# Scores of a cross-attention from four stacks of rounded and remainder rows, three batches ahead, in place of two stacks of plain rows, two batches ahead

## The chip, the core and the metric

The kernel runs on one core of a Trainium2 chip. The metric is the time on the device, in microseconds (us), of one execution. TensorE (PE) multiplies and has a weight load beside it (PEld); VectorE (DVE), ScalarE (ACT) and GpSimd (POOL) do the rest; SyncE (SP) issues most DMAs.

## What is computed

Four layers over `x` (16 batches of 128 rows of 128) with a context of 16 x 120 rows: a cross-attention with 16 heads of 8, a mixture of 16 experts of which each row takes 4, a second cross-attention with one head, and a feed-forward layer whose two square maps are butterflies. All of the change lies in the first:

```python
q = (x @ Wq.T + bq).reshape(B, N, HEADS, HEAD_DIM).transpose(0, 2, 1, 3)
k = (context @ Wk.T + bk).reshape(B, M, HEADS, HEAD_DIM).transpose(0, 2, 1, 3)
v = (context @ Wv.T + bv).reshape(B, M, HEADS, HEAD_DIM).transpose(0, 2, 1, 3)
attn = jax.nn.softmax(jnp.einsum('bhnd,bhmd->bhnm', q, k) * scale, axis=-1)
out = jnp.einsum('bhnm,bhmd->bhnd', attn, v)
return out.transpose(0, 2, 1, 3).reshape(B, N, C) @ Wo.T + bo
```

Here `x` has been normed by row, HEADS is 16, HEAD_DIM 8, N 128, M 120. `x` then gets `tanh(g) * out` added and goes to the mixture.

## The kernel before

Every engine has one program written out by hand, and waits on semaphores. The batches form four groups of four (`G`, `GB`). There are three stages.

The start (0 to about 41 us). For each group PE computes keys (`keys0`), keys and values for the second attention (`keys1`, `both_values`), turns the normed rows (`turn_rows0`) and computes queries (`queries`); ACT takes each from its bank into SBUF. DVE has the row statistics (`row_stats0`, `variances`, `refined`) and norms the rows (`normed_rows`), with a square root on POOL between them (`inverse_root`). At the end of that DVE writes two small sums of the identity (lines 1333 and 1334, semaphore `sums_rdy`); POOL waits for them and makes from them the butterflies' first matrices (lines 356 to 398, semaphore `up_mats`). PE multiplies these (`products(..., UP_L)`, line 1022) between its first score phases.

A score is a product over 8 numbers. Keys and queries of a group leave PE as 128 partitions by columns. `stack_k` and `stack_q` fold them by DMA into `ks` and `qs`: in each of four blocks of 32 partitions 8 rows hold the 8 numbers of a head, a ninth (row `HD`) holds one for the keys and minus the row's maximum for the queries, and the rest is zero. `ks` and `qs` have room for two groups. Groups 0 and 1 are stacked from SP (half of group 0's queries from ACT) at the start. Groups 2 and 3 are stacked from POOL, in its program order: `stack(2)` stands behind the weight splits `split(0)`, `split(1)`, the bias rows `xr` and all of the second butterfly's matrices, `stack(3)` behind `split(2)` and `split(3)`; each also waits until the batches that used its half are done (`st_mm`).

The attention loop (41 to about 135 us, 16 batches). `phase(b, half)` on PE holds 16 matmuls that compute the scores of batch b transposed, for the exponential (line 931), and between them 16 that compute the scores of batch b + 2, for the maxima (line 938); both have 32 rows and 120 or 128 columns, in fp32. DVE takes the maxima (`maxima`, line 1347), PE turns them (`turn_max`, line 946), ACT copies them to `mxr` (line 694), and SP's `stack_max` (line 288) carries them by DMA to the ninth row of `qs`, for which `phase(b, 0)` waits (`mx_ld`). Then come `values` (line 957), `turn_heads` (966), `weighted` on DVE, `turn_attn` (973), `project` (977) and `residual` on DVE (1361). In one iteration PE does: phase(b, 0), turn_max(b + 1), values(b - 1), turn_attn(b - 2), phase(b, 1), project(b - 2), turn_heads(b - 1). `keep_busy` (line 1003) is a matmul of no use, with 256 columns.

POOL, after `stack(3)`, does the rest of the first butterfly (lines 406 to 412), `up_bias_stages`, `values1` four times (line 487), `norm2(0)` (lines 499 to 513) and `norm_rows(0)` (518, 520). The last gives the rows that PE turns in iteration 14 with `turn_normed(0)` (line 983).

The mixture and what follows (135 to 354.5 us) need `up` (lines 1105 to 1107), whose weights are the splits: `w1_hi` (rounded) and `w1_lo` (remainder), for which PE waits with `w1_split`. Each split is a cast and a subtraction of 128 x 1024 on POOL (lines 430, 431), with the fetch of the next but one behind it (line 330).

## Time and profile before

| | us |
|---|---|
| median of 3 runs | 356.65 (356.06 to 357.22) |
| the profiled execution | 356.27 |
| its span, first to last instruction | 354.5 |
| PE busy in the span | 314.1 (89%) |
| DVE, ACT, POOL busy | 240.3, 211.8, 159.5 |

Between the profiled execution and its span lie 1.8 us. The busy shares are means over stages with different limits, so what a change of one stage is worth is read in that stage: in the list of instructions in order of time, in the waits of a stretch, and in the clock granted to PE there.

### The profile page before, as it was taken

The numbers are of one execution on the slowest core, as the hardware profiler recorded it, in microseconds if no ns is written. First come the engines' busy times: TensorE is split into PE (matmuls) and PEld (weight loads), VectorE is DVE, ScalarE is ACT, GpSimd is POOL, SyncE is SP. The second block draws the span as 40 slices with busy tenths as digits, with TensorE's granted clock in tenths as the row PEclk, the third lists the DMA queues.
The fourth block names the chain that finished last, engine by engine and source line by source line (L and its number), as shares of the span: only waits on it lengthen the run. The fifth ranks groups of instructions, "written<-read, shape, count | busy, mean of one in ns | idle before, by whom it ended". The sixth has DMA issues, their size and how long they took to land.

```text
span 354.5 us, 7313 instructions
## 1 busy us (share of the span) xinstructions
PE 314.1 (89%) x2654; PEld 222.9 (63%) x2654; DVE 240.3 (68%) x603; ACT 211.8 (60%) x411; POOL 159.5 (45%) x254
## 2 busy tenths in 40 slices
PE   4768998839798998999999978999889998999986
PEld 2435777637677776666666645765656665646866
DVE  5672556625566464969998978788958888758251
ACT  3545366615456576685658666668676566764733
POOL 3358998991998021317936340046200394312020
PEclk9999999969899999999999999999999999999999
DMA  7958220120430004323322223413223332000100
GB/s 232 201 70 186 74 66 4 32 35 4 66 121 7 6 2 138 134 89 112 131 93 87 91 88 86 124 46 108 90 92 115 92 108 97 5 1 3 59 31 30
DMA packets 15091, 27.93 MB, mean 79 GB/s; under 512 B 2552, under 2 KB 4040, under 8 KB 15048
## 3 DMA queue, kind: packets, MB, share of 16 engines
q1 hardware_dynamic: 12720, 23.00, 22.2%
q0 software_dynamic: 1408, 3.18, 4.1%
q10 hardware_dynamic: 928, 1.29, 1.3%
q8 instruction: 21, 0.34, 0.4%
q14 instruction: 14, 0.11, 0.1%
HBM read 24.05 MB, written 1.18 MB: 71 GB/s over the span
## 4 chain that ended last, share of the span: by engine, by line
PE 51%; POOL 14%; DVE 13%; issue 8%; ACT 8%; DMA 5%; SPq 1%; ACTq 0%; DVEq 0%; POOLq 0%
PE bank L1116 10%; PE bank L1105 5%; PE bank L1107 5%; PE bank L1106 5%; PE bank L1226 4%; PE bank L931 4%; PE bank L957 3%; PE bank L1211 3%; DMA x_sb<-in_x 3%; DVE rings L1533 3%; DVE rings L1536 2%; POOL xr L442 1%; POOL w_lo L431 1%; DMA rings<-mxr 1%; ACT rings L792 1%
## 5 line engine op out<-in xcount | busy, mean ns | idle before, releaser
L1105 PE MATMUL bank<-xhl,w_hi 128*128 128x512 f32 x128 | 74.9, 585 | 0.8 <-ACT rings L792 0.8
L792 ACT ACTIVATE rings<-bank,cols 128x512 f32<-128x512 f32 x64 | 44.1, 689 | 49.2 <-PE bank L1107 48.9
L1347 DVE TENSOR_REDUCE nt<-bank 128x4 f32<-128x480 f32 x64 | 39.9, 650 | 40.0 <-PE bank L938 40.0
L1533 DVE SCALAR_TENSOR_TENSOR rings<-rings,gates 128x512 f32<-128x512 f32 x64 | 47.4, 740 | 16.9 <-ACT rings L792 16.6
L1107 PE MATMUL bank<-xhl,w_hi 128*128 128x512 f32 x128 | 50.5, 394 | 0.0
L1106 PE MATMUL bank<-xhl,w_lo 128*128 128x512 f32 x128 | 50.3, 393 | 0.0
L931 PE MATMUL bank<-rings,ks 32*120 32x128 f32 x512 | 38.4, 289 | 10.5 <-DMA rings<-rings 6.4
L796 ACT ACTIVATE rings<-bank,b1c 128x512 f32<-128x512 f32 x64 | 44.0, 688 | 0.5
L931 PEld LDWEIGHTS bank<-rings,ks 32*120 32x120 f32 x512 | 32.3, 186 | 15.9 <-issue 12.4
L938 PE MATMUL bank<-ks,rings 32*128 32x120 f32 x512 | 38.9, 291 | 1.3 <-DVE nt L1347 0.7
L1105 PEld LDWEIGHTS bank<-xhl,w_hi 128*128 128x128 f32 x128 | 24.1, 188 | 18.1 <-ACT rings L792 7.9
L1106 PEld LDWEIGHTS bank<-xhl,w_lo 128*128 128x128 f32 x128 | 24.2, 189 | 17.1 <-issue 14.4
L938 PEld LDWEIGHTS bank<-ks,rings 32*128 32x128 f32 x512 | 32.8, 194 | 2.2 <-DVE nt L1347 1.3
L1116 PE MATMUL bank<-rings,x_sb 128*128 128x512 f32 x64 | 33.1, 598 | 0.0
L1536 DVE TENSOR_SCALAR rings<-rings 128x512 f32<-128x512 f32 x64 | 33.0, 515 | 0.1
L1116 PE MATMUL bank<-wide,x_sb 128*128 128x512 f32 x64 | 32.7, 592 | 0.0
L1107 PEld LDWEIGHTS bank<-xhl,w_hi 128*128 128x128 f32 x128 | 24.0, 187 | 5.7
L533 POOL TENSOR_TENSOR xhl<-xnt,xhl 128x512 fp32r<-128x512 f32 x4 | 5.7, 1422 | 48.3 <-ACT xhl L709 27.1
L1541 DVE TENSOR_TENSOR rings<-rings 128x512 f32<-128x512 f32 x32 | 24.2, 757 | 4.2
L1541 DVE TENSOR_TENSOR wide<-rings 128x512 f32<-128x512 f32 x32 | 22.8, 713 | 4.6 <-DVE rings L1536 0.5
L339 POOL TENSOR_TENSOR cs<-cs,minus_half 128x4 f32<-128x4 f32 (+1 forms) x5 | 7.2, 1437 | 34.9 <-DVE cs L1292 34.9
L685 ACT ACTIVATE wide<-bank 120x512 f32<-120x512 f32 x32 | 17.1, 584 | 6.0 <-PE bank L931 6.0
(247 smaller groups left out, 625.9 us busy)
## 6 DMA issues: line engine op xcount, KB each, us to landing
gates<-gate_rows SPq DMA_DIRECT2D x64, 256.0 KB, 3.1
bw<-in_L_ffn_w POOLq DMA_DIRECT2D x4, 512.0 KB, 5.3
x_sb<-in_x SPq DMA_DIRECT2D x4, 256.0 KB, 7.7
x_sb<-in_L_ffn_w SPq DMA_DIRECT2D x2, 512.0 KB, 4.3
wide<-in_ctx ACTq DMA_DIRECT2D x4, 240.0 KB, 6.8
out<-xr SPq DMA_DIRECT2D x3, 256.0 KB, 2.1
gates<-in_flies SPq DMA_DIRECT2D x1, 704.0 KB, 7.0
rings<-rings POOLq DMA_DIRECT2D x8, 64.0 KB, 4.5
```

The source lines that it names most:

```text
L792: act.activation(esg[:, e % 2, :], SB[1 + e % 2][:, :], ACT.Gelu_apprx_sigmoid, bias=b1_in[:, 0, e:e + 1]).then_inc(s["m_sg"], 1)
L796: act.activation(eb[:, e % 2, :], (SB[3], PK)[e % 2][:, :], ACT.Identity, bias=b1c[:, e:e + 1]).then_inc(s["m_eb"], 1)
L931: mm = pe.matmul(turned_bank(b, gg)[0:M, r * P:(r + 1) * P], ks[32 * gg:32 * gg + 32, i, r, mc], qs[32 * gg:32 * gg + 32, i, r, tc], start ...
L938: mm = pe.matmul(score_bank(ahead, n)[:, r * M:(r + 1) * M], qs[rows32, ia, r, ta], ks[rows32, ia, r, ma], start=True, stop=True)
L1105: pe.matmul(bk[:, :], w1_hi[:, e, branch, :], low(g), start=True, stop=False)
L1106: pe.matmul(bk[:, :], w1_lo[:, e, branch, :], high(g), start=False, stop=False)
L1107: pe.matmul(bk[:, :], w1_hi[:, e, branch, :], high(g), start=False, stop=True).then_inc(s[done], 1)
L1116: pe.matmul(Y[:, :], w2_sb[:, e, :], es[e % len(es)], start=False, stop=(e == E - 1), skip_group_check=True).then_inc(s["m_y"], 1)
L1347: dve.tensor_reduce(nt[:, b % 2, OF[n], :], score_bank(b, n)[:, 0:HR * M].rearrange("p (r m) -> p r m", r=HR), AX.X, ALU.max, negate=True) ...
L1533: dve.scalar_tensor_tensor(eq[:, j, :], esg[:, j, :], GELU_LIMIT, gates[:, (n - 1) % NG, :], ALU.min, ALU.mult).then_inc(s["m_eq"], 1)
L1536: dve.tensor_scalar(ec[:, j, :], eb[:, j, :], LIMIT + 1.0, 1.0 - LIMIT, ALU.min, ALU.max).then_inc(s["m_ec"], 1)
L1541: dve.tensor_tensor(es[e % len(es)], eq[:, j, :], ec[:, j, :], ALU.mult).then_inc(s["m_s"], 1)
```

## The change

Each group gets stacks of its own. Keys of groups 0 and 1 lie in `w1_lo`, queries of groups 0 and 1 in `w1_hi`, keys of groups 2 and 3 in `ks`, queries of group 2 in `xhl`, of group 3 in a new `qs`. Every number now has four rows: rounded keys, rounded keys, the keys' remainder and (in the last number's place, `MAX_ROW`) the row of the maximum, against rounded queries, the queries' remainder, rounded queries. So 24 rows and one more of each 32 are used. The matmuls stay in fp32 with 32 rows. DVE computes the remainders (`low_keys`, `low_queries`, eight instructions). A stack is filled by six DMAs of 240 or 256 KB, each to every fourth partition, all from SP; groups 2 and 3 are stacked in the first batches of the loop, after POOL has filled and zeroed their slots. Since the slots lie in the weights' tiles, POOL splits all four quarters of the weights only once batch 7 is through (`halves`). Scores are computed three batches ahead of their use instead of two. Six `keep_busy` are added in the last batches. The probabilities of the second attention and two hidden tiles of the last layer move to other tiles (`p1`, `p1t`, `hid`; not shown).

```diff
 
 
+    MAX_ROW = 3
+    AHEAD = 3
...
-        ks = sb("ks", [P, 2, HR, GB * M])
+        ks = sb("ks", [P, 2, HR * GB * M], F32R)
...
+        qs = sb("qs", [P, HR * GT], F32R)
...
-        kt_row = sb("kt_row", [P, G, GB * M])
...
+        KSLOT, QSLOT = HR * GB * M, HR * GT
+        k_rows = (w1_lo_row[:, 0:KSLOT], w1_lo_row[:, KSLOT:2 * KSLOT], ks[:, 0, :], ks[:, 1, :])
+        q_flat = (w1_hi_row[:, 0:QSLOT], w1_hi_row[:, QSLOT:2 * QSLOT],
+                  xhl[:, :, :].rearrange("p s c -> p (s c)"), qs[:, :])
+        k_slot = [v.rearrange("p (r u m) -> p r u m", r=HR, u=GB) for v in k_rows]
+        q_slot = [v.rearrange("p (r u t) -> p r u t", r=HR, u=GB) for v in q_flat]
+        q_lo = ring_row[:, 0:2 * GT].rearrange("p (i t) -> p i t", i=2)
+        k_lo = ring_row[:, 2 * GT:2 * GT + 2 * GB * M].rearrange("p (i t) -> p i t", i=2)
+        kt_row = ring_row[:, 4 * GT:4 * GT + G * GB * M].rearrange("p (g t) -> p g t", g=G)
...
+        def stacked(eng, slot, row, src, landed):
+            eng.dma_start(slot[row:P:4].bitcast(F32), src).then_inc(s[landed], 16)
...
-            sp.wait_ge(s["ks_fill"], 1)
-            sp.wait_ge(s["kt_rdy"], 1)
-            stack_k(sp, 0, range(HG))
+            def stack_k(g):
+                if g < 2:
+                    sp.wait_ge(s["ks_fill"], g + 1)
+                else:
+                    sp.wait_ge(s["kb_fill"], g - 1)
+                sp.wait_ge(s["kt_rdy"], g + 1)
+                stacked(sp, k_slot[g], 0, kt_row[:, g, :], f"ks_ld{g}")
+                stacked(sp, k_slot[g], 1, kt_row[:, g, :], f"ks_ld{g}")
+                sp.wait_ge(s["kl_rdy"], g + 1)
+                stacked(sp, k_slot[g], 2, k_lo[:, g % 2, :], f"ks_ld{g}")
+
+            def stack_q(g):
+                sp.wait_ge(s["qs_zero"], g + 1)
+                sp.wait_ge(s["qt_rdy"], g + 1)
+                stacked(sp, q_slot[g], 0, q_rows[g], f"qs_ld{g}")
+                stacked(sp, q_slot[g], 2, q_rows[g], f"qs_ld{g}")
+                sp.wait_ge(s["ql_rdy"], g + 1)
+                stacked(sp, q_slot[g], 1, q_lo[:, g % 2, :], f"qs_ld{g}")
...
+            stack_k(0)
             sp.dma_start(flies, a["flies"]).then_inc(s["ld_fly"], 16)
-            sp.wait_ge(s["qs_zero"], 1)
-            sp.wait_ge(s["qt_rdy"], 1)
...
-            stack_k(sp, 1, range(HG))
+            stack_q(0)
+            stack_k(1)
             sp.dma_start(mats[:, W_T, :].rearrange("p (c d) -> p c d", c=HC), a["L1_ffn_W_exp"]).then_inc(s["ld_exp"], 16)
...
-            stack_q(sp, 1, range(HG))
+            stack_q(1)
...
             def stack_max(b):
                 sp.wait_ge(s["mxr_rdy"], b + 1)
-                sp.dma_start(qs[HD:P:32, (b // GB) % 2, :, b % GB * P:(b % GB + 1) * P], mxr[:, b % 2, :]
+                sp.dma_start(q_slot[b // GB][MAX_ROW:P:32, :, b % GB, :].bitcast(F32), mxr[:, b % 2, :]
                              ).then_inc(s[f"mx_ld{b % 2}"], 16)
 
             for b in range(NB):
                 stack_max(b)
+                if b in (0, 2):
+                    stack_k(2 + b // 2)
+                if b in (1, 3):
+                    stack_q(2 + b // 2)
...
-            pool.memset(qs[:, 0, :, :], 0.0).then_inc(s["qs_zero"], 1)
+            pool.memset(q_flat[0].bitcast(F32), 0.0).then_inc(s["qs_zero"], 1)
...
-            pool.memset(qs[:, 1, :, :], 0.0).then_inc(s["qs_zero"], 1)
+            pool.memset(q_flat[1].bitcast(F32), 0.0).then_inc(s["qs_zero"], 1)
...
+            for g in range(2, G):
+                pool.tensor_copy(k_rows[g], which[:, MAX_ROW:MAX_ROW + 1].to_broadcast([P, KSLOT])).then_inc(s["kb_fill"], 1)
+                pool.memset(q_flat[g].bitcast(F32), 0.0).then_inc(s["qs_zero"], 1)
...
-            split(0)
-            split(1)
...
-            def stack(g):
-                pool.wait_ge(s["ks_fill"], 2)
-                pool.wait_ge(s["kt_rdy"], g + 1)
-                pool.wait_ge(s["qt_rdy"], g + 1)
...
-            stack(2)
-            split(2)
-            split(3)
-            stack(3)
...
+
+            def halves():
+                pool.wait_ge(s["st_mm"], 2 * GB * HG)
+                for q in range(NQ):
+                    split(q)
...
             up_bias_stages()
+            halves()
             for i in range(G):
...
-                act.activation(kt_row[:, g, :], bank[4][:, 0:GB * M], ACT.Identity,
+                act.activation(kt_row[:, g, :].bitcast(F32R), bank[4][:, 0:GB * M], ACT.Identity,
...
             keys0(2)
             queries(0)
-            act.wait_ge(s["qs_zero"], 1)
-            act.wait_ge(s["qt_rdy"], 1)
-            stack_q(act, 0, range(HG // 2, HG))
...
@@ -728,13 +734,14 @@
             act.wait_ge(s["consts"], 1)
             turned_max(0)
             taken("up_mm1", mats[:, HALFWAY, :], PO[:, :], "up_ev1")
+            turned_max(1)
...
                     taken("ub_mm2", ubx[:, 0, :], PO[:, 0:HC], "ub_rdy")
-                if b + 1 < NB:
-                    turned_max(b + 1)
+                if b + 2 < NB:
+                    turned_max(b + 2)
...
-                    pe.wait_ge(s["kt_rdy"], g)
+                    pe.wait_ge(s["kl_rdy"], g)
...
                 if g >= 1:
-                    pe.wait_ge(s["qt_rdy"], g)
...
-                ahead = b + 2
+                ahead = b + AHEAD
...
-                    i, mc, tc = rows_of(b)
+                    k_, q_, u = k_slot[b // GB], q_slot[b // GB], b % GB
...
                     if ahead % GB == 0 and half == 0:
-                        pe.wait_ge(s[f"ks_ld{ahead // GB}"], 16 * HG)
-                        pe.wait_ge(s[f"qs_ld{ahead // GB}"], 16 * (HG + ahead // (2 * GB)))
+                        pe.wait_ge(s[f"ks_ld{ahead // GB}"], 16 * 3)
+                        pe.wait_ge(s[f"qs_ld{ahead // GB}"], 16 * 3)
                     need(pe, "nt_rdy", ahead * HG + 2 * half - 1)
...
-                            mm = pe.matmul(turned_bank(b, gg)[0:M, r * P:(r + 1) * P], ks[32 * gg:32 * gg + 32, i, r, mc],
-                                           qs[32 * gg:32 * gg + 32, i, r, tc], start=True, stop=True)
+                            mm = pe.matmul(turned_bank(b, gg)[0:M, r * P:(r + 1) * P], k_[32 * gg:32 * gg + 32, r, u, :].bitcast(F32),
+                                           q_[32 * gg:32 * gg + 32, r, u, :].bitcast(F32), start=True, stop=True)
...
-                            mm = pe.matmul(score_bank(ahead, n)[:, r * M:(r + 1) * M], qs[rows32, ia, r, ta],
-                                           ks[rows32, ia, r, ma], start=True, stop=True)
+                            mm = pe.matmul(score_bank(ahead, n)[:, r * M:(r + 1) * M], qa[rows32, r, ua, :].bitcast(F32),
+                                           ka[rows32, r, ua, :].bitcast(F32), start=True, stop=True)
...
             def turn_max(b):
                 pe.wait_ge(s["nt_rdy"], (b + 1) * HG)
-                need(pe, "x1_rdy", b - 3)
+                need(pe, "mxr_rdy", b)
+                need(pe, "x1_rdy", b - 4)
...
             def values(b):
 
                 pe.wait_ge(s["exp_rdy"], (b + 1) * HG)
                 pe.wait_ge(s["v_st"], b + 1)
                 need(pe, "on_rdy", b)
+                if b >= NB - AHEAD:
+                    keep_busy(PO, 1)
...
             def turn_attn(b):
                 pe.wait_ge(s["on_rdy"], b + 1)
-                pe.wait_ge(s["mxr_rdy"], min(b + 4, NB))
+                pe.wait_ge(s["mxr_rdy"], min(b + 5, NB))
                 need(pe, "x1_rdy", b)
+                if b >= NB - AHEAD:
+                    keep_busy(TP, 1)
                 pe.transpose(TP[:, 0:P], on[:, :, :].rearrange("p h d -> p (h d)"), ident[:, :]).then_inc(s["on_turned"], 1)
...
-            phase(-2, 0)
+            phase(-3, 0)
...
+            pe.wait_ge(s["ql_rdy"], G)
+            phase(-3, 1)
+            phase(-2, 0)
             pe.wait_ge(s["v_rdy"], 2 * G)
             turn_max(0)
...
             products(PO, UP_L, lambda c: chunk(W_T, c), "up_mm1")
             keep_busy(bank[3], 1)
+            phase(-2, 1)
+            phase(-1, 0)
+            turn_max(1)
             phase(-1, 1)
-            pe.wait_ge(s["kt_rdy"], G)
+            pe.wait_ge(s["kl_rdy"], G)
             pe.wait_ge(s["bo_rdy"], 1)
...
                 phase(b, 0)
-                if b + 1 < NB:
-                    turn_max(b + 1)
+                if b + 2 < NB:
+                    turn_max(b + 2)
...
+            dve.tensor_copy(k_rows[0], keys_of).then_inc(s["ks_fill"], 1)
+
+            def low_keys(g):
+                dve.wait_ge(s["kt_rdy"], g + 1)
+                if g >= 2:
+                    dve.wait_ge(s[f"ks_ld{g - 2}"], 16 * 3)
+                dve.scalar_tensor_tensor(k_lo[:, g % 2, :].bitcast(F32R), bank[4][:, 0:GB * M], bcol[:, CK0:CK0 + 1],
+                                         kt_row[:, g, :], ALU.add, ALU.subtract).then_inc(s["kl_rdy"], 1)
+
+            def low_queries(g):
+                dve.wait_ge(s["qt_rdy"], g + 1)
+                if g >= 2:
+                    dve.wait_ge(s[f"qs_ld{g - 2}"], 16 * 3)
+                dve.scalar_tensor_tensor(q_lo[:, g % 2, :].bitcast(F32R), bank[2][:, :], bcol[:, CQ0:CQ0 + 1],
+                                         q_rows[g], ALU.add, ALU.subtract).then_inc(s["ql_rdy"], 1)
...
             row_stats0(0)
             own.wait()
             variances(GB, stats[:, 0:GB, :], mean[:, 0:GB])
-            dve.tensor_copy(ks[:, 1, :, :], keys_of).then_inc(s["ks_fill"], 1)
+            dve.wait_ge(s["ld_kb"], 16)
+            low_keys(0)
+            dve.tensor_copy(k_rows[1], keys_of).then_inc(s["ks_fill"], 1)
             for g in range(1, G):
                 row_stats0(g)
             refined(1, GB, rr[:, 0:1, 0:GB])
             normed_rows(0)
             own.wait()
             variances(NB - GB, stats[:, GB:NB, :], mean[:, GB:NB])
+            low_keys(1)
             refined(2, NB - GB, rr[:, 0:1, GB:NB])
-            for g in range(1, G):
-                normed_rows(g)
+            normed_rows(1)
+            low_queries(0)
+            low_keys(2)
+            normed_rows(2)
+            normed_rows(3)
+            low_queries(1)
+            low_keys(3)
             own.mark(dve.tensor_reduce(in_block, ident[:, :].rearrange("p (b j) -> p j b", b=NBLK), AX.X, ALU.add))
             dve.tensor_reduce(of_block, ident[:, :].rearrange("p (b j) -> p b j", b=NBLK), AX.X, ALU.add).then_inc(s["sums_rdy"], 1)
...
             maxima(0, 0)
             maxima(0, 1)
+            low_queries(2)
+            low_queries(3)
             row_bias()
             maxima(0, 2)
             maxima(0, 3)
+            for n in range(HG):
+                maxima(1, n)
             for n in range(HG - 1):
-                maxima(1, n)
+                maxima(2, n)
             for b in range(NB + 2):
-                if b + 1 < NB:
-                    maxima(b + 1, HG - 1)
+                if b + 2 < NB:
+                    maxima(b + 2, HG - 1)
                 if b >= 2:
                     weighted(b - 2)
-                if b + 2 < NB:
+                if b + AHEAD < NB:
                     for n in range(HG - 1):
-                        maxima(b + 2, n)
+                        maxima(b + AHEAD, n)
```

## Rows read from the trace of the kernel before

**Rows 1.** The page, first line: the span.
```profile
span 354.5 us, 7313 instructions
```
**Rows 2.** Waits between 66 and 80 us: who waited for whom, us, times, longest.
```profile
PE bank L931 <- DMA rings<-rings: 6.4, 1, 6.4
```
**Rows 3.** Chain that ended last, 60 to 135 us: start, us, what.
```profile
89.33 4.58 DMA rings<-mxr
```
**Rows 4.** DVE in order of time: `residual` of one batch; start, us, instruction.
```profile
69.93 0.34 DVE L1361 SCALAR_TENSOR_TENSOR xr<-bank,tg,xr 128x128 f32<-128x128 f32 x1
...
82.48 0.34 DVE L1361 SCALAR_TENSOR_TENSOR xr<-bank,tg,xr 128x128 f32<-128x128 f32 x1
...
92.31 0.34 DVE L1361 SCALAR_TENSOR_TENSOR xr<-bank,tg,xr 128x128 f32<-128x128 f32 x1
...
99.84 0.34 DVE L1361 SCALAR_TENSOR_TENSOR xr<-bank,tg,xr 128x128 f32<-128x128 f32 x1
...
119.50 0.34 DVE L1361 SCALAR_TENSOR_TENSOR xr<-bank,tg,xr 128x128 f32<-128x128 f32 x1
```
**Rows 5.** Stretches: window, length, busy us by engine, PE's granted clock, DMA share, GB/s.
```profile
76.00:79.00 3.00, 2.67 (x41) 2.25 (x45) 0.57 (x1) 0.25 (x2) 2.86 (x3) 0.50 0.00 0
...
94.00:96.00 2.00, 2.00 (x33) 1.79 (x33) 0.03 (x1) 0.00 (x0) 1.84 (x3) 0.50 0.12 12
```
**Rows 6.** DVE in order of time, 18 to 40 us.
```profile
21.59 3.17 DVE L1311 TENSOR_SCALAR rings<-x_sb,mean,rr 128x128 f32<-128x128 f32 x12
...
24.95 0.28 DVE L1334 TENSOR_REDUCE sums<-ident 128x8 f32<-128x128 f32 x1
```
**Rows 7.** POOL in order of time, 24 to 37 us.
```profile
25.29 0.24 POOL L415 COPY ones_low<-sums 128x64 f32<-128x64 f32 x1 [3.23 <-DVE sums L1334]
...
35.44 1.05 POOL L398 TENSOR_TENSOR mats<-blocks,sums 128x512 f32<-128x512 f32 x1
```
**Rows 8.** SP's queue in order of time: four DMAs of one stack.
```profile
20.37 2.81 SPq L239 DMA_DIRECT2D ks<-kt_row  x4
```
**Rows 9.** The page, DMA issues: KB of each, us from issue to landing.
```profile
bw<-in_L_ffn_w POOLq DMA_DIRECT2D x4, 512.0 KB, 5.3
...
out<-xr SPq DMA_DIRECT2D x3, 256.0 KB, 2.1
```
**Rows 10.** A stretch in which the old stack of group 1 is carried.
```profile
22.00:24.00 2.00, 0.66 (x4) 0.42 (x4) 2.00 (x9) 1.34 (x3) 0.06 (x1) 1.00 0.56 62
```
**Rows 11.** PE in order of time, 33 to 42 us.
```profile
36.12 1.15 PE L938 MATMUL bank<-ks,rings 32*128 32x120 f32 x16 [0.74 <-DVE nt L1347]
...
37.32 1.06 PE L1022 MATMUL bank<-mats 128*128 128x128 f32 x8
38.21 0.60 PE L1003 MATMUL bank<-wt,ident 128*128 128x256 f32 x2
...
41.35 0.36 PE L931 MATMUL bank<-rings,ks 32*120 32x128 f32 x1
```
**Rows 12.** DVE's groups by line and shape: busy us, mean ns.
```profile
L1524 DVE SCALAR_TENSOR_TENSOR xr<-bank,tg,xr 128x512 f32<-128x512 f32 x3 | 2.3, 751 | 1.3 <-PE bank L1226 1.1
```
**Rows 13.** POOL in order of time: two splits, then 60 to 165 us.
```profile
36.56 1.04 POOL L430 CAST w_hi<-bw 128x1024 fp32r<-128x1024 f32 x1
...
40.93 1.05 POOL L430 CAST w_hi<-bw 128x1024 fp32r<-128x1024 f32 x1
...
100.98 4.96 POOL L487 TENSOR_TENSOR v_all<-v_all,rows 120x512 f32<-120x512 f32 x4
...
113.54 1.04 POOL L520 TENSOR_TENSOR xn<-xn,rr 128x512 f32<-128x512 f32 x1
```
**Rows 14.** PE in order of time, 119 to 141 us.
```profile
120.90 0.60 PE L983 MATMUL bank<-ident,xn 128*128 128x128 f32 x4
...
132.78 1.08 PE L957 MATMUL bank<-wide,vst 120*32 120x128 f32 x32 [0.56 <-DVE on L1355]
...
134.53 0.49 PE L977 MATMUL bank<-wt,ont 128*128 128x128 f32 x2 [0.40 <-ACT ont L698]
```

55 lines of the change are left out of this document (15 added, 40 removed).

## The prediction

> **What bounds the kernel now.** I read the page first: PE is busy for 89% of a span of 354.5 us [rows 1], and the change touches only the first 135 us, so the mixture behind them is taken as it is. Then I looked for the places where the attention loop is late. `residual` runs once in a batch, so its starts are the loop's beat [rows 4]: from 99.84 to 119.50 lie four batches, 4.92 us each, and from 82.48 to 92.31 two, again 4.92. But 69.93 to 82.48 is one batch (12.55, too long by 7.6), and so is 92.31 to 99.84 (7.53, too long by 2.6). The waits name the first: PE stood 6.4 us for the DMAs of group 2's stack [rows 2], which POOL issued late. The chain names the second: one DMA of a row of maxima that took 4.58 us [rows 3] while group 3's stack was carried. After each stall PE's clock was at half (0.50, the 1.2 GHz level) [rows 5]; that loss is inside the two excesses. Together the loop loses 10.2 us. That is all that the change can win here: its matmuls keep type, rows and columns.
>
> Then the start. The first loop phase begins at 41.35 [rows 11]. POOL's matrices need 25.29 to 36.49, 11.2 us [rows 7], and POOL begins when DVE has made the two sums, at 25.23 [rows 6]. PE is there at about the same time as the matrices (37.32) [rows 11], so POOL's chain can't slip without being seen.
>
> **The loop, minus 10.2.** All four stacks have slots of their own and SP issues the last two around batches 0 to 3; `phase(5, 0)`, the first to read group 2, comes 25 us after the loop's start (five beats). Both stalls go: the first because nobody waits for POOL, the second because a row of maxima is now turned a whole batch earlier, so its DMA has 4.9 us more. The beat stays 4.92: phase, turn, values and the DVE steps keep their order and only the batch number of the scores ahead changes. In batch 13 the scores ahead fall away; DVE has four maxima less in a batch that it helps to pace. I take 0.5 off (between 0 and 1.0, an estimate), since the 16 matmuls that are left run almost as long.
>
> **The start, plus 8.9.** This is the term that I am least sure of. `low_keys(3)` stands ahead of the two sums on DVE and waits until all three key DMAs of group 1 have landed. Queued behind it on DVE are the sums, and on them wait POOL's matrices, and on these PE. Step by step:
> - `low_queries(0)` comes after `normed_rows(1)`, a third of 3.17 us after 21.59, so at 22.65 [rows 6]. A remainder over 512 columns with one operand in PSUM costs 0.75 by the nearest row [rows 12]; done at 23.4. Eight of these add 6 us to DVE, nearly all in idle time of the start; what they cost is where they wait.
> - SP then issues the last query DMA of group 0 and the three key DMAs of group 1 in its order. An old one takes 0.70 us of SP [rows 8]; the last starts at 25.5.
> - Landing: the near bound is 2.1 us for 256 KB from an idle queue [rows 9], so 27.6. The far bound is volume: these four carry 976 KB, and the old stack ran at 62 GB/s with the engines at 0.56 [rows 10], 111 GB/s if full, thus 8.8 us from 24.5, 33.3. I take 28.6, near the first, because the old DMAs each wrote to 8 neighbouring partitions and the new ones write to 32 spread over all 128.
> - Remainder 0.75 and sums 0.6: POOL starts at 30.0 instead of 25.3, its matrices are ready at 41.2. PE by then has done everything up to `turn_max(0)` by about 38.4 (the remainders of group 3's queries hold its second phase until 35) and idles for some 3 us.
> - From the matrices on, before, it was 4.03 us to the first loop phase (37.32 to 41.35) [rows 11]. Now two more phases stand there, each 1.15 plus 0.74 of waiting for a maximum, 1.89 [rows 11]: 7.8 us, so 49.0. Stalls of this kind cost the clock in two places above; I add 1.2 for it. The loop starts at 50.2, 8.9 late. Bounds: 4.9 late if the matrices come by 38.4 and the clock holds; 14 late at the far bound.
>
> Here the Trainium skill is to be weighed ("SBUF — State Buffer", section on the DMA port swizzle). Its rule is that a DMA's rate grows with how many of 16 ports its partitions reach, and that 8 neighbouring ones reach two, while every fourth of 128 reaches all. With its fit of 2 us plus bytes at 436 GB/s the key DMAs would land at about 27.8 and the start would slip by 0.8 less, for a time of 356.3, called an estimate. The row with 62 GB/s for the old form agrees with the rule's direction; no row shows the new form.
>
> **The end of the loop, plus 2.2.** A `keep_busy` costs 0.60 us of PE [rows 11], and PE does them after its wait, so they lengthen the path. Six make 3.6. PE idles 0.56 and 0.40 there [rows 14], and DVE paces part of it, which may swallow some. I take 2.2, between 0 and 3.6.
>
> **POOL's splits, plus 0.4.** They start after phase(7, 1). What POOL must do until PE can turn the first normed rows in batch 14: two splits with the issue of a fetch behind them at 4.37 (40.93 minus 36.56), two without at 3.5, and 1.2 us of waiting for the two fetches, which take 5.3 each [rows 9, 13]; then values, norms and rows, 100.98 to 114.58, 13.6 [rows 13]. That is 8.7 + 7.0 + 1.2 + 13.6 = 30.5 us. PE needs seven beats less the 2.9 us between a turn and the end of its second phase, less the 0.5 above: 31.1. Before, the rows were ready 6.3 us early (114.58 against 120.90) [rows 13, 14]; now half a microsecond is left. That cover is thin, so 0.4 (0 to 2). The fills and zeroing for groups 2 and 3 and all that POOL moves ahead of the splits end near 80, before batch 7 does (88), and cost nothing.
>
> SP: the key stacks of groups 2 and 3 stand ahead of rows of maxima and wait for POOL's fills (43 to 47). The row of batch 1 is then issued near 47 and needed at 55; nothing.
>
> **Sum.** 356.27 (profiled execution, 1.8 over its span [rows 1]) - 10.2 - 0.5 + 8.9 + 2.2 + 0.4 = 357.1. The profiled execution lies 0.4 under the median 356.65, so this is 0.1% above the median: no change that could be measured. A measurement of this kernel can tell about 0.3% (1.1 us) from none.
>
> **Rivals.**
> - *The matrices hardly slip.* If the key DMAs land by 27.6, something holds DVE less, and the clock holds, the start is 4.9 late and the `keep_busy` are partly swallowed (1.5): 352.0, up to 354.5 between. For it: nothing but small steps has to go right. Against: the sum above has the matrices at 41.2, and this needs 38.4. I give it 0.22, at 352.5.
> - *The key DMAs land late* (slower). Place: DVE's wait in `low_keys(3)`. Each microsecond beyond 28.6 moves the loop by one. At 33 the start is some 13 late: 361.2. It decides from about 30 on. For it: three times the old volume, 1920 byte pieces. Chance 0.13.
> - *The splits are late.* Place: `turn_normed(0)` waiting for POOL in batch 14. Each microsecond beyond 31.1 is paid; with 3 late, 360. It decides if a split takes over 4.5 us or a fetch over 6. Chance 0.12.
> - *The change doesn't do what it says:* a stack or a row of maxima still comes late in batches 1 to 5, since 3 MB pass SP's queue there. With half of the stalls back, 362. Chance 0.05.
> - The forecast, 357.1, own range 355 to 359.5, keeps 0.48: of that 0.10 is faster by over 0.3% (under 355.6), 0.20 within, 0.18 slower.
>
> Faster: 0.22 + 0.10 = 0.32. Same: 0.20. Slower: 0.18 + 0.13 + 0.12 + 0.05 = 0.48. The range goes from 352.3, which cuts off the better half of the first rival, to 361.5, which cuts off half of the second and the fourth.
>
> **What would show it.** In the changed profile: `residual` at a beat of 4.92 from batch 2 to 13 with no gap over 6; the line of the two sums at 29 to 30 instead of 24.7; the last matrix at 41; the first transposed scores at 50, with a clock of 0.50 between; the four splits from about 88; the turning of normed rows with a short wait for POOL. Wrong it would be if the sums come at once (the start then is only bound by PE), if the beat itself changes with the new rows, or if the mixture's 219 us move.

## The result and the profile after

| | before | after |
|---|---|---|
| median of 18 runs each, us | 356.36 | 360.55 (358.20 to 367.17) |
| the profiled execution, us | 356.27 | 359.00 |
| its span, us | 354.5 | 357.2 |
| mean granted clock of it | 0.986 | 0.975 |

The changed kernel is slower: 1.0096 times the kernel before, 95% interval 1.0066 to 1.0126, some 3.4 us. Medians are of all executions; a ratio leaves out slow ones, more than 1.5% above the fastest of their kernel. 357.1 was forecast, in a range of 352.3 to 361.5. The range held, and the forecast lies 3.5 us under the median. The profiled execution of after is one of its better ones, 1.6 us under that median, so the ledger below explains 2.7 us of span and not all of the 4.2 us between the medians.

The page of after, its first line, PE's line and the clock by fortieths of the span (8.9 us each):
```profile
span 357.2 us, 7348 instructions
...
PE 323.5 (91%) x2666; PEld 230.2 (64%) x2666; DVE 246.0 (69%) x611; ACT 212.3 (59%) x411; POOL 154.8 (43%) x240
...
PEclk9999669999999999999999998999999999999999
```
PE is busy for 9.4 us more than before, and the two sixes, from 36 to 54 us, are where much of that comes from: the same matmuls at half the clock.

`residual` on DVE (start, us), to be laid beside [rows 4]: batches 0, 10 and 15 of the kernel before, then batches 0, 10, 11 and 15 of after, where its line is 1395:
```profile
55.17 0.34 DVE L1361 SCALAR_TENSOR_TENSOR xr<-bank,tg,xr 128x128 f32<-128x128 f32 x1
...
114.59 0.34 DVE L1361 SCALAR_TENSOR_TENSOR xr<-bank,tg,xr 128x128 f32<-128x128 f32 x1
...
138.40 0.35 DVE L1361 SCALAR_TENSOR_TENSOR xr<-bank,tg,xr 128x128 f32<-128x128 f32 x1 [2.19 <-PE bank L977]
```
```profile
65.73 0.34 DVE L1395 SCALAR_TENSOR_TENSOR xr<-bank,tg,xr 128x128 f32<-128x128 f32 x1
...
114.90 0.34 DVE L1395 SCALAR_TENSOR_TENSOR xr<-bank,tg,xr 128x128 f32<-128x128 f32 x1
119.62 0.35 DVE L1395 SCALAR_TENSOR_TENSOR xr<-bank,tg,xr 128x128 f32<-128x128 f32 x1 [3.01 <-PE bank L992]
...
140.61 0.35 DVE L1395 SCALAR_TENSOR_TENSOR xr<-bank,tg,xr 128x128 f32<-128x128 f32 x1 [2.62 <-PE bank L992]
```
From batch 0 to batch 10 these are 49.17 us, ten beats of 4.92 with no gap. Before it was 55.17 to 114.59, 59.42: the stalls of 10.25 us are gone, as forecast (10.2). But batch 0 comes 10.56 us later than before. At batch 10 the two kernels are level (+0.31). The end of the loop, with the six fillers (the `keep_busy` matmuls of the last batches), adds 1.90 (batch 15: 138.40 before, 140.61 now, +2.21), and 0.5 comes behind the loop, which makes the 2.7 us of span.

The start, on DVE and POOL, beside [rows 6] and [rows 7]:
```profile
26.89 0.72 DVE L1297 SCALAR_TENSOR_TENSOR rings<-bank,cols,rings 128x480 fp32r<-128x480 f32 x1 [1.03 <-DMA w_lo<-rings]
27.53 0.36 DVE L1367 TENSOR_REDUCE sums<-ident 128x16 f32<-128x128 f32 x1
...
28.14 0.24 POOL L432 COPY ones_low<-sums 128x64 f32<-128x64 f32 x1 [6.96 <-DVE sums L1368]
...
38.25 1.05 POOL L415 TENSOR_TENSOR mats<-blocks,sums 128x512 f32<-128x512 f32 x1
```
`low_keys(3)` waited 1.03 us for the key DMAs, which landed at about 26.9. The matrices are ready at 39.30, 2.81 us later than before, where 4.7 was forecast.

The same on PE, beside [rows 11]:
```profile
36.02 2.07 PE L942 MATMUL bank<-w_lo,w_hi 32*128 32x120 f32 x16 [0.74 <-DVE nt L1381]
39.36 2.08 PE L1031 MATMUL bank<-mats 128*128 128x128 f32 x8 [0.96 <-POOL mats L415]
...
46.20 2.06 PE L942 MATMUL bank<-w_lo,w_hi 32*128 32x120 f32 x16 [0.54 <-DVE nt L1381]
48.19 2.08 PE L1031 MATMUL bank<-mats 128*128 128x128 f32 x8
...
51.05 0.56 PE L935 MATMUL bank<-w_hi,w_lo 32*120 32x128 f32 x1
```
A score phase of 16 matmuls took 1.15 us before and 2.07 here, eight products 1.06 to 1.16 before and 2.08 here. The stretch from 30 to 36, first of the kernel before, then of after (length, busy us by engine, clock, DMA share, GB/s):
```profile
30.00:36.00 6.00, 4.08 (x30) 2.79 (x28) 0.94 (x3) 2.52 (x5) 5.14 (x16) 1.00 0.80 186
```
```profile
30.00:36.00 6.00, 3.20 (x26) 2.04 (x24) 2.03 (x6) 1.80 (x4) 5.28 (x16) 0.98 0.67 205
```
More stretches of after:
```profile
36.00:38.00 2.00, 1.98 (x16) 1.78 (x16) 0.54 (x1) 0.00 (x0) 1.61 (x8) 0.50 0.06 25
...
40.00:42.00 2.00, 2.00 (x9) 1.57 (x8) 0.00 (x0) 0.53 (x1) 2.00 (x2) 0.50 0.02 8
...
44.00:46.00 2.00, 1.36 (x17) 1.06 (x17) 1.32 (x3) 0.30 (x2) 2.00 (x2) 1.00 0.23 84
46.00:48.00 2.00, 1.80 (x16) 1.78 (x16) 0.71 (x2) 0.26 (x2) 2.00 (x3) 0.51 0.08 27
48.00:50.00 2.00, 2.00 (x12) 1.81 (x9) 1.22 (x2) 0.00 (x0) 2.00 (x3) 0.50 1.00 371
```
Twice the clock is at 0.50 (the 1.2 GHz level): from 36 to 42, after 30 to 36 in which PE was busy for 3.20 of 6 us, and from 46 to 52, after 44 to 46 with 1.36 of 2. In the profiled execution of before it was 1.00 from 30 to 52, with PE busy for 4.08 us from 30 to 36.

The splits on POOL, beside [rows 13], and the turn that waits for them, beside [rows 14]:
```profile
89.81 1.04 POOL L451 CAST w_hi<-bw 128x1024 fp32r<-128x1024 f32 x1 [12.68 <-PE bank L935]
...
119.36 1.04 POOL L529 TENSOR_TENSOR xn<-xn,rr 128x512 f32<-128x512 f32 x1
```
That is 30.6 us from the first split to the normed rows (30.5 forecast). PE turned them at 121.01, 0.6 us after they were ready, with no wait.

### The profile page after: what moved, and what is told of

It is laid out like the page before. It is cut to its first block, busy times and chain, and to the rows that moved or that the text cites. A ratio compares the mean times of both kernels' runs of the same rounds, so it can differ in the third digit from the quotient of the medians.

```text
span 357.2 us, 7348 instructions
## 1 busy us (share of the span) xinstructions
PE 323.5 (91%) x2666; PEld 230.2 (64%) x2666; DVE 246.0 (69%) x611; ACT 212.3 (59%) x411; POOL 154.8 (43%) x240
## 3 DMA queue, kind: packets, MB, share of 16 engines
q10 hardware_dynamic: 848, 1.15, 1.0%
## 4 chain that ended last, share of the span: by engine, by line
PE 62%; DVE 15%; issue 9%; ACT 7%; POOL 4%; DMA 2%; SPq 0%; DVEq 0%; ACTq 0%; POOLq 0%
PE bank L1128 11%; PE bank L935 6%; PE bank L1117 6%; PE bank L1118 5%; PE bank L1119 5%; PE bank L970 5%; PE bank L1238 4%; PE bank L1223 3%; DVE rings L1571 3%; DVE nt L1381 2%; DMA x_sb<-in_x 2%; PE bank L942 2%; PE bank L956 2%; PE bank L1031 2%; DVE rings L1574 2%
## 5 line engine op out<-in xcount | busy, mean ns | idle before, releaser
L1128 PE MATMUL bank<-rings,x_sb 128*128 128x512 f32 x64 | 34.0, 613 | 0.0
L942 PE MATMUL bank<-w_lo,w_hi 32*128 32x120 f32 x256 | 21.4, 312 | 3.4 <-DVE nt L1381 2.0
L942 PEld LDWEIGHTS bank<-w_lo,w_hi 32*128 32x128 f32 x256 | 18.2, 214 | 4.9 <-DVE nt L1381 2.6
L691 ACT ACTIVATE rings<-bank 120x512 f32<-120x512 f32 x32 | 17.1, 584 | 6.2 <-PE bank L935 6.2
L935 PE MATMUL bank<-w_hi,w_lo 32*120 32x128 f32 x256 | 19.1, 288 | 1.5 <-DVE nt L1381 1.5
```

Source lines behind the costliest of these rows:

```text
L935: mm = pe.matmul(turned_bank(b, gg)[0:M, r * P:(r + 1) * P], k_[32 * gg:32 * gg + 32, r, u, :].bitcast(F32), q_[32 * gg:32 * gg + 32, r, u ...
L942: mm = pe.matmul(score_bank(ahead, n)[:, r * M:(r + 1) * M], qa[rows32, r, ua, :].bitcast(F32), ka[rows32, r, ua, :].bitcast(F32), start=T ...
L1128: pe.matmul(Y[:, :], w2_sb[:, e, :], es[e % len(es)], start=False, stop=(e == E - 1), skip_group_check=True).then_inc(s["m_y"], 1)
```

## The experiments

Each was timed in five rounds. Four series were run, each with the kernel before beside it (its medians: 356.5 for e1 to e4, 356.6 for e5 to e8, 357.5 for e9 to e11, 356.3 for e12). "Ratio" is that of the times to the kernel before, with its 95% interval. "Clock" is the mean granted clock of the profiled execution, and "batch 0" is where `residual` starts for batch 0 in it. A difference between two medians of different series can be off by about 1 us: the median of the kernel before moved by that much.

| run | median, us | ratio | clock | batch 0 |
|---|---|---|---|---|
| changed kernel | 360.55 | 1.0096 [1.0066, 1.0126] | 0.975 | 65.73 |
| e1 sums first | 360.52 | 1.0117 [1.0076, 1.0159] | 0.975 | 65.80 |
| e2 gaps filled | 354.89 | 0.9967 [0.9938, 0.9996] | 0.995 | 60.96 |
| e3 no fillers at the end | 357.93 | 1.0051 [1.0024, 1.0077] | 0.976 | 65.42 |
| e5 e2 and e3 | 352.39 | 0.9901 [0.9862, 0.9939] | 0.999 | 60.67 |
| e8 e5, values later | 351.76 | 0.9881 [0.9847, 0.9916] | 0.994 | 60.94 |
| e6 two ahead | 353.47 | 0.9913 [0.9879, 0.9946] | 0.984 | 58.67 |
| e9 e6, gaps filled | 350.58 | 0.9841 [0.9798, 0.9883] | 0.995 | 57.16 |
| e10 e9, no fillers at the end | 348.44 | 0.9771 [0.9731, 0.9810] | 0.990 | 57.38 |
| e7 rounded products | 371.90 | 1.0403 [1.0349, 1.0457] | 0.866 | 63.57 |
| e4 before, stack early | 350.02 | 0.9811 [0.9756, 0.9865] | 0.979 | 62.59 |
| e11 the same again | 352.44 | 0.9841 [0.9781, 0.9901] | 0.980 | 62.56 |
| e12 before, gaps filled | 355.90 | 0.9988 [0.9957, 1.0019] | 0.986 | 58.52 |

**e1: is it the slip of the matrices?** The two sums go ahead of the remainders that wait.

```diff
+            own.mark(dve.tensor_reduce(in_block, ...))
+            dve.tensor_reduce(of_block, ...).then_inc(s["sums_rdy"], 1)
             low_queries(1)
             low_keys(3)
-            own.mark(dve.tensor_reduce(in_block, ...))
-            dve.tensor_reduce(of_block, ...).then_inc(s["sums_rdy"], 1)
```

> The changed kernel, with DVE's two sums ahead of the last two remainders instead of behind them. The theory (the late start is the clock's doing, the matrices' slip costs only the 1 us that PE waits for them): POOL begins at about 25 instead of 28.1, the matrices are ready by 36.5, PE waits for them no more, and the first loop phase comes 1 to 1.5 us earlier than at 51.05 with the clock still at its 1.2 GHz level in two stretches; time 359 against 360. The rival (the matrices' chain paces the whole start, as forecast): the first loop phase comes some 2.8 us earlier, near 48; time 357. A third possibility: with the 1 us wait gone the clock doesn't fall the first time, and the gain is 3 or more; then the clock row between 36 and 42 us tells it.

The sums came at 24.48, as early as before, and nothing was gained: 360.52. PE in order of time in this kernel:
```profile
35.28 1.63 PE L942 MATMUL bank<-w_lo,w_hi 32*128 32x120 f32 x16 [3.08 <-DVE rings L1304]
37.64 2.06 PE L942 MATMUL bank<-w_lo,w_hi 32*128 32x120 f32 x16 [0.74 <-DVE nt L1381]
```
The wait for the matrices is replaced by one for the remainders of the queries, now longer (3.08 where it was 1.34), and the clock was at half in the same two places. The edit moved more than the sums. POOL's two weight fetches of 512 KB stand behind them, and were issued at 25.80 instead of 28.84; the last query DMA of group 1, issued at 26.38, then took 8.0 us to landing (3.7 in after), and the remainder of group 3's queries waited for it until 34.47 (33.32 in after). So e1 shows a second chain that is as late as the matrices. It doesn't show that the matrices' slip costs nothing, and e2 and e9 below show that it does cost.

**e2: is it the clock?** Seven fillers go into the gaps.

```diff
+            keep_busy(bank[3], 2)
             pe.wait_ge(s["ql_rdy"], G)
             phase(-3, 1)
+            keep_busy(bank[3], 1)
             phase(-2, 0)
+            keep_busy(bank[3], 1)
             pe.wait_ge(s["v_rdy"], 2 * G)
             turn_max(0)
+            keep_busy(bank[3], 1)
...
             phase(-2, 1)
+            keep_busy(bank[3], 1)
             phase(-1, 0)
+            keep_busy(bank[3], 1)
             turn_max(1)
             phase(-1, 1)
```

> The changed kernel, with seven useless matmuls of 256 columns put into the places between 32 and 47 us where PE waits for maxima, remainders or matrices. The theory (PE's clock falls to its 1.2 GHz level because these early phases are paced by DVE and leave PE idle, and half speed makes the start long): granted clock 1.00 from 34 to 54 us, first loop phase at about 47 instead of 51.05, time 355.5 to 356. The rival (the start is long because two phases, their maxima and the late matrices stand in it, the clock matters little): each filler costs its 0.5 us where it isn't hidden, first loop phase at 51 to 53, time 360 to 362.

Seven matmuls of no use made the kernel 5.6 us faster by the medians (4.6 by the ratios). Stretches of this kernel:
```profile
34.00:40.00 6.00, 4.86 (x46) 3.68 (x47) 2.89 (x6) 0.27 (x1) 5.31 (x13) 1.00 0.07 28
40.00:46.00 6.00, 5.88 (x62) 4.39 (x61) 2.74 (x5) 1.16 (x4) 6.00 (x4) 1.00 0.35 124
46.00:52.00 6.00, 6.00 (x93) 5.06 (x92) 3.18 (x6) 2.95 (x8) 5.89 (x7) 1.00 0.59 218
```
The clock is 1.00 throughout, a phase takes 1.15 us again, and batch 0 comes 4.77 earlier. This shows the cause of the late start beyond the work itself. PE in order of time around the matrices and the three phases behind them:
```profile
39.20 1.16 PE L1035 MATMUL bank<-mats 128*128 128x128 f32 x8 [1.03 <-POOL mats L415]
...
40.73 1.15 PE L942 MATMUL bank<-w_lo,w_hi 32*128 32x120 f32 x16
...
42.62 1.15 PE L942 MATMUL bank<-w_lo,w_hi 32*128 32x120 f32 x16
...
44.52 1.15 PE L942 MATMUL bank<-w_lo,w_hi 32*128 32x120 f32 x16
```
Two things can be read here. With the clock held PE still waits 1.03 us for the matrices, and starts their products 1.88 later than before (39.20 against 37.32 [rows 11]). And the phases are 1.89 and 1.90 us apart with a filler between them, as far apart as the forecast had them without one, so those fillers lie wholly in the gaps.

A small part of the gain is lost again later. PE in order of time in batch 14 of this kernel:
```profile
117.03 0.65 PE L998 MATMUL bank<-ident,xn 128*128 128x128 f32 x4 [0.73 <-POOL xn L529]
```
PE waits for the normed rows behind POOL's splits. POOL's chain took 31.9 us here, since two fetches were waited for (0.92 and 1.61 us; 0.77 and 0.47 in after).

**e3: the six fillers at the end.** The four lines of `keep_busy` in `values` and `turn_attn` are left out.

> The changed kernel without the six useless matmuls in the last three batches. Theory of the forecast (they lie on the path and cost 2.2 us): the first matmul of the mixture comes about 1.8 us earlier after residual(10), the third pair about 2.2, and the time falls to 358. The rival (they hold the clock up): without them the granted clock falls below 1.00 between 118 and 142 us and the time stays at 360 or rises.

357.93, so 2.6 us less. A stretch of this kernel:
```profile
118.00:142.00 24.00, 21.24 (x257) 17.44 (x256) 10.78 (x47) 15.46 (x35) 6.49 (x10) 1.00 0.15 49
```
The clock is 1.00 without them, so in this kernel they kept nothing up. In the profile the stretch from batch 11 to 15 is 1.07 shorter (119.33 to 139.25, against 119.62 to 140.61), with a late chain on POOL once more (32.1 us, and PE waited 0.91 us for it). Between the later pair e9 and e10, where POOL is not late, the same edit gives 2.04 (111.24 to 132.19, against 111.46 to 130.37).

**e5 and e8: both together, and POOL's chain without `values1`.** e5 has the edits of e2 and e3. e8 also has POOL compute `values1` behind `norm_rows(0)`.

> The changed kernel with the early gaps filled and without the six useless matmuls of the last batches: two edits together that gave 5.6 and some 2 us alone. If they add up, 353. The theory of POOL's splits says that they don't quite: with the loop at its full beat the normed rows of batch 14 come late, PE waits 0.7 to 1.3 us for them before it turns them (it was 0.73 with the gaps filled), and the time is 353 to 354.

> The same as e5_gaps_no_tail, with one step moved: POOL adds the bias to the second attention's values (4 x 1.24 us) after the normed rows of group 0 instead of before them. If POOL's chain of splits is what PE waits for in batch 14, the wait goes, residual(11) to residual(12) falls by 1 us or more, and the time is 1 us under e5_gaps_no_tail, 352 to 352.5. The rival (that wait is covered by other work of the last batches, which PE does in its place): both times equal.

352.39: the two gains add up. With `values1` out of the way, the normed rows are ready 4.8 us earlier (111.05 against 115.81), and from batch 11 to 12 it takes 6.62 us where e5 took 6.61. So in e5's profile POOL wasn't on the path (31.1 us from the first split, no wait on PE), and the times of e5 and e8 lie within each other's intervals. This says nothing of executions with later fetches.

**e6: was the third batch ahead needed?**

```diff
-    AHEAD = 3
+    AHEAD = 2
...
-            phase(-3, 0)
+            phase(-2, 0)
...
-            phase(-3, 1)
-            phase(-2, 0)
+            phase(-2, 1)
+            phase(-1, 0)
...
-            phase(-2, 1)
-            phase(-1, 0)
-            turn_max(1)
             phase(-1, 1)
...
-                if b + 2 < NB:
-                    turn_max(b + 2)
+                if b + 1 < NB:
+                    turn_max(b + 1)
```
(`maxima`, `turned_max` and the bounds of the waits go with it; the fillers of the last three batches stay.)

> The changed kernel with scores two batches ahead again instead of three; stacks, rows and useless matmuls of the end as in the change. Theory of the forecast: the third batch costs the start two phases of 1.89 us, and buys only cover for the rows of maxima. So the loop starts at about 46 to 47 instead of 51.05, and PE waits for rows of maxima in batches 1 to 4, while SP's queue carries the stacks of groups 2 and 3; if these waits stay under 4 us in all, the time is 356 to 358. The rival (the cover is needed): waits for rows of maxima of 6 us and more, clock down again in the loop, time 361 or above.

7.1 us less, where no more than 4.5 was expected. The beat is 4.92 from batch 0 to batch 11, and no wait for a row of maxima is among PE's waits: the waits expected in batches 1 to 4 didn't come. SP issues each late stack right behind a row of maxima (the row at 46.55, three query DMAs from 47.23, the next row at 51.69), and no row came late by it. So with these stacks the order didn't have to change. Stretch of this kernel where the clock still falls:
```profile
38.00:42.00 4.00, 3.04 (x13) 2.29 (x11) 1.22 (x2) 0.82 (x3) 3.85 (x4) 0.50 0.01 4
```

**e9 and e10: two ahead with the gaps filled, then without the fillers at the end.** Five fillers: two before the wait for `ql_rdy`, one behind each of the two phases that follow, one behind `turn_max(0)`.

> The changed kernel with two batches ahead instead of three, and five fillers of 128 x 256 in the gaps of its start (in the three-ahead kernel seven such fillers gave 5.6 us). Theory (of the 7 us that two ahead gave, a part was the second fall of the clock and the rest the two phases): one stretch at 0.50 is left in the two-ahead kernel, and in it a phase takes 2.07 instead of 1.15, the products 2.08 instead of 1.16 and the filler 1.06 instead of 0.6. With the gaps filled the clock stays at 1.00 and the first residual row comes at about 56.5 instead of 58.67; the time is about 351.5 us. Rival (the two-ahead kernel waits in its start for POOL's products of matrices and for the remainders of the keys, whatever the clock): the first residual row stays at 58.5 or later and the time at 353.5.

> As the two-ahead kernel with its gaps filled, and without the six fillers of the last three batches. Theory (each of these fillers lies on the path, some 0.3 us each, as it did with three ahead, where leaving them out gave 2.5 us beside the filled gaps): about 2 us less than the same kernel with them, 349.5 us, so 0.98 of the kernel before. Rival (with the score phases of batch 14 and 15 thinner, PE gaps let the clock fall in the last batches): the clock shows 0.5 to 0.8 in the stretch from batch 13 to the first matmul of the mixture, and the time is no less than with the fillers.

350.58 and 348.44: e10 beats both kernels, 0.977 of the kernel before. PE in order of time in e9, the products of the matrices and the first loop phase:
```profile
39.20 1.16 PE L1034 MATMUL bank<-mats 128*128 128x128 f32 x8 [1.03 <-POOL mats L415]
...
43.33 0.36 PE L934 MATMUL bank<-w_hi,w_lo 32*120 32x128 f32 x1
```
With the clock at 1.00 in both, e9 and e2 differ by the third batch ahead and two fillers: 60.96 less 57.16 is 3.80, the very figure forecast for the two phases (e2 shows the two fillers in gaps). In time it is 4.3 us. Batch 0 of e9 is 2.0 behind that of the kernel before. Of that 1.88 is there when PE starts the products of the matrices: with the clock held, the late matrices are all but all that the new stacks cost the start. e9's batch 0 was expected at 56.5 and came at 57.16. Of the fall of the clock that e10's rival expected at the end there was a little (0.93 on the mean of 120 to 140, where e9 has 1.00), and e10 was still 2.1 us faster than e9.

**e7: rounded operands.** In the four operands of the score matmuls `.bitcast(F32)` is left out, so they are read as the rounded type in which they are stored.

> The changed kernel with the score matmuls reading the stacks as the rounded type in which they are stored, instead of as fp32: same rows, same columns, nothing left out. One view (PE's fp32 work is the beat of the loop): the 32 matmuls of a phase, 1.1 us in fp32, take a half or less, and the beat falls from 4.92 to some 4; time 345 or below. The other view (the beat is the ring of DVE's maxima, ACT's exponentials and PE together): the beat falls by less than 0.3, PE has more idle time, the clock falls more often, and the time stays within 2 us of 360.

371.90, so 11.4 us slower than the changed kernel, and outside of both views. A stretch of its loop, then one of PE's groups in 60 to 120 us (busy us, mean ns), and in the third fence the same group of after in 66 to 116:
```profile
60.00:70.00 10.00, 9.87 (x123) 7.33 (x115) 4.91 (x12) 5.84 (x17) 9.53 (x10) 0.50 0.01 3
```
```profile
L970 PE MATMUL bank<-wide,vst 120*32 120x128 f32 x164 | 10.1, 420 | 0.7
```
```profile
L970 PE MATMUL bank<-wide,vst 120*32 120x128 f32 x160 | 5.4, 275 | 1.0 <-DVE on L1389 1.0
```
The beat is 6.02 instead of 4.92 and the clock 0.50 from 60 to 130, nearly to the end of the loop, although PE's row shows it busy for 9.87 of 10 us; `values`, which e7 doesn't touch, has its mean at 420 ns instead of 275. Once down, the loop came back up only behind 130. Why a loop so busy by the profile stays down I can't say: no run tells it apart from other differences of the type, and so the run doesn't show what the rounded type would give with the clock up.

**e4 and e11: the kernel before with one thing moved.**

```diff
+            stack(2)
             own.then_wait(across(wdn_flat, dw2[:, 0, :, :], 2))
             across(wdn_flat, dw2[:, 1, :, :], 1).then_inc(s["dn_crossed"], 1)
             pool.wait_ge(s["dn_crossed"], 1)
...
-            stack(2)
             split(2)
```

> The kernel before, with one edit: on POOL the stack of group 2 stands ahead of the last two steps on the second butterfly's matrices instead of behind them. It isolates the first stall. Theory (the stall of 6.4 us is POOL's program order alone, with the clock behind it): POOL issues the stack at about 61 as soon as batch 3 is through, PE doesn't wait in iteration 6, residual(3) to residual(4) takes 4.9 to 6 us instead of 12.55, and the time falls by some 7 us, to 349.5. The rival (the stack's DMAs, beside the rows of maxima, move the stall to another batch): a wait for a row of maxima of 2 to 4 us appears between 62 and 70, and the gain is 3 to 5 us.

> The kernel before, with nothing of the change but that POOL stacks its last group ahead of the two crossings of the down matrix. Its time is known (350.0 us); wanted is an undisturbed trace of it. Theory (the stalls of the kernel before were POOL's order, not its one stack): from the row of batch 8 to that of batch 9 about 6 us instead of 12.55, of which about 1.6 is a wait for the row of maxima, the first residual row at 55.2 as in the kernel before, and the six stalls of 10.2 us shrunk to some 3.5. Rival (the gain came from elsewhere, the start or the tail): the distances between the rows of batches 0 and 10 are as in the kernel before, and a stretch outside them is shorter.

350.0 and 352.4: two plain stacks with POOL's order mended are 8 to 10.5 us better than the changed kernel, and 0.981 and 0.984 of the kernel before. `residual` in e11, PE's waits in 60 to 110 us, and the issue of group 2's stack by POOL:
```profile
72.39 0.34 DVE L1361 SCALAR_TENSOR_TENSOR xr<-bank,tg,xr 128x128 f32<-128x128 f32 x1
78.38 0.34 DVE L1361 SCALAR_TENSOR_TENSOR xr<-bank,tg,xr 128x128 f32<-128x128 f32 x1
83.30 0.34 DVE L1361 SCALAR_TENSOR_TENSOR xr<-bank,tg,xr 128x128 f32<-128x128 f32 x1
```
```profile
PE bank L931 <- DMA rings<-mxr: 3.2, 2, 1.6
```
```profile
67.64 2.29 POOL L239 DMA_DIRECT2D ks<-kt_row  x4 [6.13 <-PE bank L931]
```
These rows are of batches 2, 3 and 4. From batch 3 to 4, where the kernel before lost 12.55 [rows 4], it is 4.92 here; a gap of 5.99 stands one batch earlier and one of 6.01 from batch 6 to 7, each a wait of 1.6 for a row of maxima. But both profiles caught an execution whose clock had fallen in the start (in e11 0.65 in 26 to 30, 0.63 in 38 to 42, 0.50 in 42 to 46), with batch 0 at 62.6. There POOL, though it waited 6.13 us for batch 3, issued the stack no earlier than in the kernel before (67.84), and PE was late enough not to need it sooner. So the traces don't show the edit at work; its worth is shown by the times. The five executions with a clock of 0.989 or more took 347.5 to 350.9, those near 0.980 took 351.6 to 355.7. And the start of the kernel before can lose its clock too.

**e12: fillers for the kernel before.** The same five as in e9.

> The kernel before with the same five fillers of 128 x 256 in the gaps of its start that the two-ahead kernel was given. It divides the 5.6 us that fillers gave the changed kernel. Theory A (the kernel before also loses the clock in the start of most of its executions: their mean granted clock is 0.976 at the median and 0.986 in the profiled one, while 0.99 to 1.00 was seen in every kernel with filled gaps): clock 0.99 or more, about 353 us, 0.99 of the kernel before; then the three-ahead change with both starts filled (354.9) costs about 2 us by its own work, and its stalls of 10 us are paid back with 12. Theory B (only the changed kernel's start is thin enough for the clock to fall): the fillers are added work here, some 0.6 us each where there is no gap, the clock stays at 0.976 to 0.986, and the time is 356.5 to 358; then the fall of the clock is the change's own, and is all of its loss.

No change: 0.9988 [0.9957, 1.0019]. `residual` in e12, and PE in order of time:
```profile
58.52 0.34 DVE L1365 SCALAR_TENSOR_TENSOR xr<-bank,tg,xr 128x128 f32<-128x128 f32 x1
...
73.27 0.34 DVE L1365 SCALAR_TENSOR_TENSOR xr<-bank,tg,xr 128x128 f32<-128x128 f32 x1
83.62 0.34 DVE L1365 SCALAR_TENSOR_TENSOR xr<-bank,tg,xr 128x128 f32<-128x128 f32 x1
...
118.74 0.34 DVE L1365 SCALAR_TENSOR_TENSOR xr<-bank,tg,xr 128x128 f32<-128x128 f32 x1
```
```profile
77.75 0.34 PE L931 MATMUL bank<-rings,ks 32*120 32x128 f32 x1 [4.46 <-DMA rings<-rings]
```
I had expected one of two things and got a third. Batch 0 is 3.35 us later than in the profile of before, yet batch 11 is 0.76 earlier (118.74 against 119.50). Not all of the 3.35 is the fillers' doing: PE was 1.33 late at 25.44, ahead of the first of them, with a clock of 0.72 from 18 to 22. The first stall has shrunk by 2.2 (10.35 against 12.55), the second by 1.9 (5.62 against 7.53). The stack that PE waits for is issued by POOL at its own time, 68.44 here and 67.84 before. So what happens to the start of the kernel before is hidden in its two stalls, as far as they reach.

## Why the prediction was right, and where its terms were off

**The stalls (forecast -10.2, measured -10.25).** Right in size. For the first stall the cause was right too: PE waits for no stack in after, and e4 and e11 gain 5.1 to 6.5 us against the median of the kernel before by POOL's order alone. For the second the reason given wasn't the one that counts: "a row of maxima is now turned a whole batch earlier", but e6 turns it no earlier and has no wait. Before, it was the row that was carried beside POOL's stack of group 3 that came late (4.58 us [rows 3]); which property of the new stacks spares the rows, their form, their queue or their time, no run takes apart.

**The slip of the matrices (4.7 forecast, 2.8 measured; in PE's start of the products 3.9 forecast, 2.0 measured).** Mis-sized: the landing. I took 28.6 for the last key DMA, with bounds from 27.6 to 33.3, and it landed at about 26.9, below them all. SP had issued all three by 25.0: the last one started at 24.4 where I had 25.5, and took 2.5 us to landing where I had 3.1. SP's queue in order of time in after:
```profile
23.14 1.86 SPq L249 DMA_DIRECT2D w_lo<-rings  x3
```
"POOL's chain can't slip without being seen" holds: of the slip of 2.81, 0.83 was slack before (36.49 to 37.32), and the rest, 1.98, is about what e9 is late with the clock held (1.88). I had looked only at the sums, though: e1 shows the remainders of the queries as late.

Here the rule of the Trainium skill that the prediction weighed ("SBUF — State Buffer", section on the DMA port swizzle) came nearer than my choice. The estimate worked out from its fit was 27.8, nearer to 26.9 than the 28.6 that I took; my near bound from a row, 27.6, was nearer still. The trace agrees with the rule, for it now shows the new form: in 48 to 50 us of after, where nothing else but three DMAs of group 2's queries was carried, it moved 371 GB/s with the engines full (the stretch above), against 62 GB/s at a share of 0.56 for the old form [rows 10], which is 111 at a full share.

**Two more phases (3.8 forecast, 3.80 measured at full clock, e2 against e9).** Right.

**The clock in the start (1.2 forecast, some 4.7 measured).** This is the step that failed. From the first product to the loop it took 11.69 us (39.36 to 51.05) instead of 4.03: 7.66 more, of which 3.8 is the two phases, so some 3.9 is clock and waits, and 0.9 more comes until batch 0. e2, with its fillers' own time included, wins 4.8 of it back. I had read two places with a clock of 0.50 [rows 5], each behind a stall, and charged the start a lump for it, without laying out PE's gaps there: the gap of 1.34 before the phase at 34, 0.74 before the next, then 0.96. Laid out, they show PE busy for half of 30 to 36, where it was busy for two thirds before (4.08 of 6). The start as a whole came out at 10.56 against the 8.9 forecast: 2.0 for the matrices instead of 3.9, 3.8 for the phases, and 4.7 for clock and waits instead of 1.2. One term was 1.9 too large and the other 3.5 too small. That the sum is near is partly luck.

**The fillers at the end (2.2 forecast, 2.04 to 2.6 measured).** Right. In e3 they guard nothing, for the clock is 1.00 without them; in e10 it fell to 0.93 from 120 to 140, and leaving them out paid even so.

**Batch 13 (-0.5 forecast, -0.2 measured):** 4.72 from batch 10 to 11 instead of 4.91.

**POOL's splits (+0.4, 0 to 2, forecast).** The chain was 30.5 by the sum and 30.6 to 32.1 in the profiles. PE waited 0 for it in after, 0.73 in e2 and 0.91 in e3, by how long two fetches took. The cover is as thin as forecast.

**What the sum left out.** It was made against one execution of before, whose clock of 0.986 is among the best of that kernel: the median of its runs of the last series has 0.976. I took a start's delay to be worth the same in both kernels. e12 shows that before the change 3.35 us of it are worth nothing, because the stalls wait for POOL's timetable and not for PE's. Taking the stalls away made every later microsecond of the start count. The runs of the changed kernel have mean clocks of 0.966 to 0.976 (all but two of 18), and those at 0.967 take about 360.5, those at 0.975 about 359. How much of the 1.6 us between its profiled execution and its median is one more stretch at half clock can't be told, as those executions left no trace.

**The rivals.** "The matrices hardly slip" came true by the landing (26.9, it needed 27.6) and only half by the matrices (39.3, it needed 38.4), and its time, 352.5, did not come, since its other condition (the clock holds) failed; with that mended, e2 has 354.9. "The key DMAs land late" and "The change doesn't do what it says" are refuted by the rows at 26.89 and by the even beat. "The splits are late" is real in some executions and below 1 us.

## What to carry to other kernels

A stall that waits for another engine's own timetable hides what comes before it. Before you book its removal as a gain, ask what it was hiding: here 10.25 us were freed, and a start longer by 10.56 took all of it; in e12 the old stalls had swallowed a start longer by 3.35 whole. If new work in a start brings waits, list PE's gaps one by one, and book the phases behind them at half clock; fillers in such gaps are cheap to try (5.6 us here), and fillers where the clock stands anyway only cost. And undo a compound change by parts: the third batch ahead cost 4 to 7 us and bought nothing. The new stacks with two batches ahead and tuned fillers (e10, 0.977, interval 0.973 to 0.981) come out little ahead of the old stacks with three lines moved on POOL (e4 and e11, 0.981 and 0.984, intervals 0.976 to 0.990), which had no fillers tried on them. So whether the stacks themselves are worth having isn't shown.
